# Attention weights kept in PSUM for every mixing sum, and the last sums placed between output chunks, in a two-layer mixer

## What is computed

```
# layer 0
att   = softmax(mlp(cond))                       # 64 x 8
agg_w = einsum('bk,koi->boi', att, weight)       # a 32x32 channel mixer per sample
y     = agg_w @ x + att @ bias_k                 # mix channels
r     = y @ base_w.T + base_b + 2 * lora(y, top-2 gates of 8)
x     = x + r
# layer 1: 9-tap grouped conv over features, plus (cond @ c_weight.T) and a
# bias, then a LoRA with top-2 gates of 4
x     = x + delta
```

## Time and profile before

| | us |
|---|---|
| median of 3 runs (199.12 to 201.44) | 199.79 |
| profiled execution, its own time | 199.16 |
| span of the profiled execution | 197.4 |
| PE busy (share of span) | 177.6 (90%) |
| DVE busy | 130.0 (66%) |
| ACT busy | 82.8 (42%) |
| POOL busy | 86.1 (44%) |

### The profile page before, as it was taken

One profiled execution on the slowest core, in us unless ns is written; L12 is line 12 of the kernel. 1 busy time (PEld: TensorE's weight loads), 2 busy tenths in 40 slices (PEclk: granted clock), 3 DMA queues, 4 the chain that ended last, 5 costly groups with the idle time before them and its releaser, 6 DMA issues.

```text
span 197.4 us, 3002 instructions
## 1 busy us (share of the span) xinstructions
PE 177.6 (90%) x1087; PEld 160.9 (81%) x1087; DVE 130.0 (66%) x251; ACT 82.8 (42%) x184; POOL 86.1 (44%) x86
## 2 busy tenths in 40 slices
PE   7999996504999899999999999999999999988991
PEld 7888886304888679999888999998889999987980
DVE  1496999996289844368877543688776753387573
ACT  3776595022082350773152517731523555126010
POOL 7023579920006672895300728952002796046000
PEclk9999999955699999999999999999999999999999
DMA  6997000001310014000002200000023000000225
GB/s 179 315 365 294 0 2 0 3 0 40 121 54 0 0 41 146 29 0 3 0 0 106 110 0 2 0 3 0 0 106 110 2 0 0 3 0 0 108 106 212
DMA packets 6350, 12.15 MB, mean 62 GB/s; under 512 B 704, under 2 KB 1088, under 8 KB 6336
## 3 DMA queue, kind: packets, MB, share of 16 engines
q1 hardware_dynamic: 6192, 11.84, 17.0%
q10 hardware_dynamic: 144, 0.13, 0.3%
HBM read 7.77 MB, written 4.19 MB: 61 GB/s over the span
## 4 chain that ended last, share of the span: by engine, by line
PE 69%; DVE 22%; ACT 3%; issue 3%; DVEq 0%; POOL 0%; ACTq 0%; POOLq 0%
PE ps L884 16%; PE ps L886 15%; PE ps L885 15%; PE ps L964 7%; DVE x1T L633 6%; PE ps L906 6%; PE ps L877 2%; DVE xs L722 2%; PE ps L961 2%; DVE xsl L627 1%; DVE late L637 1%; PE ps L1053 1%; DVE outb L710 1%; PE ps L923 1%; DVE above L609 1%
## 5 line engine op out<-in xcount | busy, mean ns | idle before, releaser
L884 PE MATMUL ps<-base_h,xTh 128*128 128x512 f32 x64 | 26.1, 408 | 0.0
L326 POOL TENSOR_TENSOR x1Tl<-x1T,x1Th 128x512 fp32r<-128x512 f32 x12 | 16.4, 1375 | 20.5 <-DVE lw L652 20.5
L886 PE MATMUL ps<-base_h,xTl 128*128 128x512 f32 x64 | 25.2, 394 | 0.0
L885 PE MATMUL ps<-base_l,xTh 128*128 128x512 f32 x64 | 25.2, 394 | 0.0
L668 DVE SCALAR_TENSOR_TENSOR x1T<-ps,side_s,xT_s 128x512 f32<-128x512 f32 x16 | 11.9, 750 | 17.0 <-PE ps L886 17.0
L310 POOL TENSOR_TENSOR xTl<-xT_s,xTh 128x512 fp32r<-128x512 f32 x12 | 15.0, 1275 | 17.2 <-ACT xTh L394 17.2
L964 PEld LDWEIGHTS ps<-mixT,p 128*128 128x128 f32 x128 | 18.9, 209 | 3.2 <-ACT p L407 1.7
L315 POOL TENSOR_TENSOR zl<-outb,zh 128x340 fp32r<-128x340 f32 x15 | 14.6, 972 | 13.5 <-ACT zh L419 13.4
L964 PE MATMUL ps<-mixT,p 128*128 128x128 f32 x128 | 19.2, 295 | 1.3 <-ACT p L407 1.3
L681 DVE TENSOR_TENSOR outb<-ps,s_sb 128x340 f32<-128x340 f32 x16 | 8.2, 510 | 17.3 <-PE ps L886 14.2
L961 PE MATMUL ps<-row_b,row_w 72*128 72x512 f32 x16 | 7.1, 442 | 10.0 <-DVE x1T L668 10.0
(11 more groups left out here) (182 smaller groups left out, 489.8 us busy)
## 6 DMA issues: line engine op xcount, KB each, us to landing
xT_s<-in_xT_dram SPq DMA_DIRECT2D x16, 256.0 KB, 4.7
out_dram<-outb SPq DMA_DIRECT2D x16, 256.0 KB, 2.3
x1T<-in_wT_dram SPq DMA_DIRECT2D x4, 256.0 KB, 6.5
x1T<-in_az_dram SPq DMA_DIRECT2D x1, 680.0 KB, 8.6
outb<-in_tapw_dram SPq DMA_DIRECT2D x1, 576.0 KB, 9.4
lgw_s<-in_lgw_dram SPq DMA_DIRECT2D x1, 272.0 KB, 3.4
...
```

Source lines behind the costliest of these rows:

```text
L326: nc.gpsimd.tensor_tensor(lo, full, hi.bitcast(F32), ALU.subtract).then_inc(x1_lo, 1)
L884: nc.tensor.matmul(dst, sh, mh, start=start and c == 0, stop=False)
L885: nc.tensor.matmul(dst, sh, ml, start=False, stop=False)
L886: last = nc.tensor.matmul(dst, sl, mh, start=False, stop=stop and c == n - 1)
```

## The change

Five things:

1. The attention weights stay in PSUM (now bank 7, `attb_b`); the copy `attb_s` is gone, and all mixing sums read PSUM. Other small products move to other banks or columns, the base sums to bank 1.
2. Mixing sum 1 moves behind `lwT_low(0)`. Sums 2 and 3 are each done in two halves of 512 results, through the tile `above`; the halves of sum 2 stand before `make_x1(0, 0)`, those of sum 3 between `make_x1(0, 0)`, `(0, 1)` and `(0, 2)`.
3. On PE the base sums move from behind chunks 2 and 3 of `x_base(0)` to ahead of them; the context product moves to the start, and the wait for the base sums' low part moves ahead of `x_logits(1, 1)`. `mix_logits(0)` now waits for both bias copies (`mixb_ok`, `ctx_ok`).
4. Loads: `side` ahead of the base weights, `az` ahead of `lbT` and of group 1's x. POOL's `uw_l` waits for `lb_lo` in place of `lw_ok`.
5. In group 1, ACT and DVE take `p0_out`, `lwT_high` and `lwT_low` ahead of part of the sums' splitting.

The diff, cut to its core:

```diff
-        attb_s = sb("attb_s", [P, TT, K0])
...
+        prod_half = above[:, 0:TG // 2 * C * K0].rearrange("p (t o k) -> p t o k", t=TG // 2, o=C)
...
-        HID, ATT, ATTT, ATTB, MXB, LGS, BSUM, CTXB, PSUMB = 7, 6, 7, 6, 7, 5, 7, 7, 7
+        HID, ATT, LGS, BSUM = 7, 6, 5, 1
+        attT_b = ps[0:K0, 6, 0:NB]
+        mixb_b = ps[:, 6, 0:NB]
+        ctx_b = ps[:, 6, NB:2 * NB]
+        attb_b = ps[:, 7, 0:TT * K0]
+        psum_b = ps[:, 7, 0:PJ]
...
+        MIX_STEPS = (1, 2, 4, 6)
+        attb = attb_b.rearrange("p (t k) -> p t k", k=K0)
...
+            sp.dma_start(side_s[:, :], side).then_inc(in_side, 16)
             for c in range(DC):
                 sp.dma_start(wT_s[:, c, :], wT[:, c, :]).then_inc(in_base[c], 16)
-            sp.dma_start(side_s[:, :], side).then_inc(in_side, 16)
+            sp.dma_start(az_s, az).then_inc(in_az, 16)
             sp.dma_start(lbT_s, lbT).then_inc(in_lb, 16)
             for c in range(DC):
                 load_xT(1, c)
-            sp.dma_start(az_s, az).then_inc(in_az, 16)
...
-            pool.wait_ge(lw_ok, 1)
+            pool.wait_ge(lb_lo, 1)
...
-            act.wait_ge(attb_mm, 1)
-            nc.scalar.activation(attb_s[:, :, :].rearrange("p t k -> p (t k)"), ps[:, ATTB, 0:TT * K0],
-                                 ACT.Copy).then_inc(attb_ok, 1)
...
-            gate_exp(0, gate0, dif0_ok, ex0_ok)
             act.wait_ge(dif_ok, 2)
             nc.scalar.activation(vw_h[:, :, :], ud, ACT.Copy).then_inc(suv_hi, 1)
+            gate_exp(0, gate0, dif0_ok, ex0_ok)
+            act.wait_ge(bsum_mm, 1)
+            nc.scalar.activation(row_w[:, :], ps[:, BSUM, :], ACT.Copy).then_inc(bsum_hi, 1)
             act.wait_ge(in_tap, 16)
             nc.scalar.activation(tap_h[:, :, :].rearrange("p k c -> p (k c)"), tapw_s, ACT.Copy).then_inc(tap_hi, 1)
             act.wait_ge(in_b1, 16)
             nc.scalar.activation(b1_h[:, :], b1T_s, ACT.Copy).then_inc(b1_hi, 1)
             for t in range(TG):
                 p0_out(0, t)
-            act.wait_ge(bsum_mm, 1)
-            nc.scalar.activation(row_w[:, :], ps[:, BSUM, :], ACT.Copy).then_inc(bsum_hi, 1)
...
             p0_out(1, 0)
+            p0_out(1, 1)
             sums_high(0, 0)
             sums_high(0, 1)
-            p0_out(1, 1)
-            sums_high(0, 2)
-            sums_high(0, 3)
             p0_out(1, 2)
             lwT_high(1)
             p0_out(1, 3)
+            sums_high(0, 2)
+            sums_high(0, 3)
...
-            def mix_sum(g, attb):
-                prod = prods[min(g, 1)]
-                if g == 1:
-                    dve.wait_ge(base_lo, DC)
-                nc.vector.tensor_tensor(prod, attb[:, TG * g:TG * (g + 1), :].unsqueeze(2).to_broadcast([P, TG, C, K0]),
-                                        wrep_s[:, :, :].unsqueeze(1).to_broadcast([P, TG, C, K0]),
+
+            def mix_sum(step, prod, t0, n):
+                nc.vector.tensor_tensor(prod, attb[:, t0:t0 + n, :].unsqueeze(2).to_broadcast([P, n, C, K0]),
+                                        wrep_s[:, :, :].unsqueeze(1).to_broadcast([P, n, C, K0]),
                                         ALU.mult).then_inc(prod_ok, 1)
-                dve.wait_ge(prod_ok, g + 1)
-                nc.vector.reduce_sum(agg[:, TG * g:TG * (g + 1), :], prod, AX_X).then_inc(agg_ok, 1)
+                dve.wait_ge(prod_ok, step)
+                nc.vector.reduce_sum(agg[:, t0:t0 + n, :], prod, AX_X).then_inc(agg_ok, 1)
+
+            def mix_half(g, half):
+                step = MIX_STEPS[g - 1] + half + 1
+                dve.wait_ge(agg_ok, step - 1)
+                mix_sum(step, prod_half, TG * g + half * TG // 2, TG // 2)
...
+            dve.wait_ge(ctx_mm, 1)
...
+            dve.wait_ge(in_side, 16)
+            for j in range(BT):
+                rows = slice(j * C, (j + 1) * C)
+                last = nc.vector.tensor_scalar(ctxbias[rows, :], ctx_b[rows, j:NB:BT],
+                                               side_s[rows, S_FS:S_FS + 1], None, ALU.add)
+            last.then_inc(ctx_ok, 1)
             for t in range(TG):
                 logits(0, t)
...
-            dve.wait_ge(agg_ok, 1)
-            mix_sum(1, attb_s)
             dve.wait_ge(bsum_hi, 1)
             minus(row_w[64:96, :], ps[64:96, BSUM, :], row_w[64:96, :]).then_inc(bsum_lo, 1)
             lwT_low(0)
-            for g in (2, 3):
-                dve.wait_ge(agg_ok, g)
-                mix_sum(g, attb_s)
-            dve.wait_ge(ctx_mm, 1)
-            dve.wait_ge(in_side, 16)
-            for j in range(BT):
-                rows = slice(j * C, (j + 1) * C)
-                last = nc.vector.tensor_scalar(ctxbias[rows, :], ps[rows, CTXB, j:NB:BT],
-                                               side_s[rows, S_FS:S_FS + 1], None, ALU.add)
-            last.then_inc(ctx_ok, 1)
-            dve.wait_ge(agg_ok, G)
+            dve.wait_ge(base_lo, DC)
+            mix_sum(2, prods[1], TG, TG)
+            mix_half(2, 0)
+            mix_half(2, 1)
             dve.wait_ge(suv_lo, 3)
-            for c in range(DC):
-                make_x1(0, c)
+            make_x1(0, 0)
+            mix_half(3, 0)
+            make_x1(0, 1)
+            mix_half(3, 1)
+            make_x1(0, 2)
+            make_x1(0, 3)
+            dve.wait_ge(agg_ok, MIX_STEPS[G - 1])
...
+            lwT_low(1)
             sums_low(0, 2)
             sums_low(0, 3)
-            lwT_low(1)
...
-                if i == 0:
-                    pe.wait_ge(attb_ok, 1)
-                elif t == 0:
+                if i and t == 0:
                     pe.wait_ge(lwT_lo, i)
...
-                    if i == 0:
-                        pe.wait_ge(bsum_lo, 1)
...
+            pe.wait_ge(in_side, 16)
+            nc.tensor.matmul(ctx_b, side_s[:, S_CTX:S_CTX + P], early_s[:, A_COND:A_COND + NB],
+                             start=True, stop=True).then_inc(ctx_mm, 1)
             pe.wait_ge(lgsum_ok, 1)
             for t in range(TG):
                 x_base(0, t, (0,))
             for t in range(TG):
                 x_base(0, t, (1,))
-            pe.wait_ge(prod_ok, 1)
+            pe.wait_ge(mixb_ok, 1)
+            pe.wait_ge(ctx_ok, 1)
             for t in range(TG):
                 mix_logits(0, t)
-            for c in range(2, DC):
-                for t in range(TG):
-                    x_base(0, t, (c,))
-            pe.wait_ge(mixb_ok, 1)
+            pe.wait_ge(base_lo, DC)
             for n, part in enumerate((base_h, base_l)):
                 for c in range(DC):
                     last = nc.tensor.matmul(ps[:, BSUM, :], ones_r[:, :], part[:, c, :],
                                             start=n + c == 0, stop=n == 1 and c == DC - 1)
             last.then_inc(bsum_mm, 1)
+            for c in range(2, DC):
+                for t in range(TG):
+                    x_base(0, t, (c,))
             turn_lw(0)
             x_logits(1, 0)
+            pe.wait_ge(bsum_lo, 1)
             x_logits(1, 1)
-            pe.wait_ge(bsum_lo, 1)
-            pe.wait_ge(in_side, 16)
-            nc.tensor.matmul(ps[:, CTXB, 0:NB], side_s[:, S_CTX:S_CTX + P], early_s[:, A_COND:A_COND + NB],
-                             start=True, stop=True).then_inc(ctx_mm, 1)
             make_y(0)
-            pe.wait_ge(ctx_ok, 1)
             pe.wait_ge(in_az, 16)
+            pe.wait_ge(prod_ok, MIX_STEPS[G - 1])
             for m in range(2):
```

More of the change, by code:

```diff
@@ L461, in mix_place @@
             def mix_place(g):
-                act.wait_ge(agg_ok, g + 1)
+                act.wait_ge(agg_ok, MIX_STEPS[g])
                 for j in range(BT):
@@ L485, in _ @@
             act.wait_ge(attT_mm, 1)
-            nc.scalar.activation(attT[:, :], ps[0:K0, ATTT, 0:NB], ACT.Copy).then_inc(attT_ok, 1)
+            nc.scalar.activation(attT[:, :], attT_b, ACT.Copy).then_inc(attT_ok, 1)
             x_high(0, 2)
@@ L529, in _ @@
             act.wait_ge(pjsum_mm, 1)
-            nc.scalar.activation(pj_sum[:, :], ps[:, PSUMB, 0:PJ], ACT.Copy).then_inc(pjsum_ok, 1)
+            nc.scalar.activation(pj_sum[:, :], psum_b, ACT.Copy).then_inc(pjsum_ok, 1)
             for t in range(TG):
```

18 lines of the change are left out of this document (8 added, 10 removed).

## The result

| | before | after |
|---|---|---|
| median of 4 runs on one chip, us | 199.45 (198.37 to 201.44) | 185.35 (184.84 to 185.81) |
| ratio after/before, 95% interval | | 0.9309, 0.9254 to 0.9364 |
| profiled execution, span, us | 197.4 | 183.7 |
| its own time, us | 199.16 | 185.67 |

The account below looks back on a forecast made before the run. PE was taken to wait 10.02 us for DVE, whose SBUF product is held by POOL, then to run at a low clock. 13.6 us there plus 1.1 at group 1 make 14.7 off 199.16: 184.7 us predicted, range 183.2 to 188.5.

Parts of the forecast that it names:

- the early stretch: PE up to the logits' end: 0.4 us for the context product, 0.4 us of wait (bounds 0 and 1.6).
- Which instructions are held: DVE beside POOL: instructions with both operands in SBUF are held; a PSUM product of 1024 takes 1.21 us.
- Rival B: DVE's PSUM products beside POOL are held like the others; only group 1's gain remains, 198.6 us; chance 0.04.
- DVE's list: DVE from ACT's lwTh at 29.3 us: lwTl 0.7, sum 1 2.5, two half sums 2.9; make_x1(0, 0) starts at 35.4.
- PE's chunks: Group 0's four output chunks: start 32.65 us, 1.87 us each, no gap, margins to DVE of 0.3 and 0 us.
- rival A: Chunks 2 and 3 of group 0: DVE misses PE by a little, 188 us, 191 with a lowered clock; chance 0.11.
- Gain up to the end of the chunks: Group 0's chunks end at 40.15 against 53.72 us, 13.6 us: 10.0 gap, 3.0 low clock and drain, 0.5 earlier start.
- signs of being wrong: A product beside POOL over 2 us, PE waiting over a us between chunks, or logits ending later than 33 us.
- Group 1's start: Ahead of group 1's first experts0: reordering removes PE's wait for ACT's tiles, 1.1 us won (bounds 0 and 1.8).
- Edits at no cost: Earlier base sums cost nothing; the removed ACT copy, reordered exponent and row_w are hidden.
- The sum: Whole kernel: 14.7 us off 199.16 gives 184.5, off the median 199.79 gives 185.1; predicted 184.7 us.

Follow-up runs that it names:

- sbuf_copy: The changed kernel with ACT's copy of the attention weights to SBUF put back and sums 1 to 3 reading it; 196.41 us, ratio 0.9915 to the kernel before.
- pool_later: The kernel before, with POOL starting group 1's bias rows and xTl only when mixing sum 3 is done; 193.45 us, ratio 0.9754.
- after_again: The changed kernel run once more without an edit; 185.56 us, ratio 0.9340 to the kernel before.
- after_third: The changed kernel run a third time without an edit, as a control; 185.80 us, ratio 0.9292 to the kernel before.
- whole_sums: The changed kernel with both halves of sum 3 ahead of make_x1(0,0); 189.11 us, ratio 0.9508 to the kernel before.
- before_again: The kernel before traced a second time without an edit; a single execution, 197.62 us, span 195.7 us.
- loads_back: The changed kernel with loads in their former order and POOL's uw_l waiting for lw_ok again; ratio 0.9263 without three slow runs, median of all six 186.69 us.
- early_y: The changed kernel with group 0's output chunk 0 waiting only for ACT's first logit copy, chunk 1 for the second; 185.29 us, ratio 0.9349.
- group1_back: The changed kernel with ACT's and DVE's order in group 1 as in the kernel before; median 187.72 us, ratio 0.9478, runs in two clusters.
- base_sums_back: The changed kernel with base sums behind chunks 2 and 3 of x_base(0) and row_w behind the base tiles again; 185.79 us, ratio 0.9362.

## Why the prediction was right

The mechanism was right and so were its large terms; one of them was in part lucky in the execution it was read from, and the early stretch was sized too small.

**Which instructions are held: right, and this decided everything.** The prediction read one row, `lwTl` at 0.69 us beside POOL's `xTl`, as the rule: a DVE instruction with one operand in PSUM isn't held, one with two in SBUF is. All five PSUM products took 1.22, 0.69 or 0.68 us. sbuf_copy gives the same instruction in the same place 10.70 us, and pool_later, with the operand left in SBUF and POOL moved, 1.21. Rival B (the PSUM products held as well, 198.6) needed a product of several us beside POOL; there is none. The Trainium skill (SBUF — State Buffer, Who interferes with whom) states that a DVE instruction with at most one SBUF input, outside the two-port modes, doesn't contend with GpSimd; the traces agree, by the 1.22 and 0.69 us above. The Trainium skill (VectorE: DVE Perf Modes, Rules for kernel authors) offers two ways for elementwise work on PSUM: to accept the rate of a PSUM source, or to copy to SBUF first if many operations follow. The second costs 12 us here: sbuf_copy is it. The changed kernel is the first, which the prediction didn't mention. Of the 62 cycles more for a PSUM source that the same page of the Trainium skill gives (The TRN2 errata) there is nothing in the rows: 1.22 against 1.22 us at 1024 results, 0.69 against 0.69 at 512.

**DVE's list: right within 0.2 us in its differences.** From ACT's `lwTh` to the first `make_x1` the prediction had 6.1 us (29.3 to 35.4); it was 36.23 - 30.31 = 5.9.

**PE's chunks: right, the margins larger than said.** 1.87 us a chunk was near (33.87 to 41.24 is 7.37 for four, 1.84 each). The start wasn't 32.65 but 33.87, with the slow start; 33.54 in after_again and 32.83 in after_third. DVE freed the first bank at 36.97 while PE wanted it at 37.59, a margin of 0.6 against the 0.3 said, the second at 38.94 against 39.41, 0.5 against 0. So rival A (DVE misses PE, 188 to 191) had some room before it. whole_sums makes it come true by another order, and 189.1 us lies between the 188 and 191 worked out for it.

**Gain up to the end of the chunks: 13.6 predicted; 12.5 in the first trace, 13.5 in after_third, 12.8 in after_again.** L1123 stood at 41.24, 40.20 and 40.90 us, predicted 40.15. The step that was mis-sized is the early stretch: the prediction took 0.4 us for the context product and 0.4 for a wait. Like for like, quick starts alone, the first base product comes 0.4 to 0.8 us later than in the kernel before (13.63 and 13.79 against 13.02 and 13.25). 0.24 of it is the context product now ahead of it, which the prediction counted (as 0.4). The rest is a wait for x, which it didn't: PE waits 0.54 us for x in after_again and 0.31 in after_third, and not at all in before_again. Why x comes later isn't shown: its loads for group 0 are issued first, at 1.72 us, in both load orders; in loads_back, with the old order, PE doesn't wait for it and the first base product starts at 13.40, but that is one trace. `ue` starts at 14.36 (first trace), 15.08 (after_again) and 14.42 us (after_third), against 13.3 to 14.2 said. The wait for `base_l`, held by `ue` as foreseen, was 0.59 us (after_again), 0.21 (early_y) and 0 (the first trace and after_third). And a slow start, which no trace of the kernel before showed, costs a further 1.2 to 1.4 us (14.98 against 13.79 and 13.63). So one of the prediction's own signs of being wrong came true: it named logits that end later than 33 us, and they end at 33.33 in the first trace, at 33.00 in after_again and at 32.30 in after_third.

**Group 1's start: 1.1 predicted, 1.33 measured.** The next thing late was `lwTl`, as said, by 0.22 us. The 14.96 us of this stretch are the same in after_again and after_third within 0.01. group1_back takes this part back and costs 3.4 us by the ratios (1.6 to 5.1 with both intervals), not 1.3, since in half of the executions the gaps seem to bring the lower clock with them. The prediction gave this part nothing for the clock, because the trace of before showed those gaps at 1.00.

**Edits at no cost: right for the base sums, open for the loads.** The place of the base sums and of `row_w` is worth nothing that these runs can tell (base_sums_back). For the load order the trace of loads_back shows nothing either, but three of its six runs are some 3 us longer. The removed copy on ACT was not tested by itself.

**The sum.** 184.7 against a median of 185.35. The difference, 0.65 us, is within the interval of the measurement (0.9254 to 0.9364 of 199.45 us is 184.6 to 186.8), so the medians alone ask for no explanation. For the profiled execution the sum was 184.5, its own time is 185.67: the chunks end 1.09 us later than said (41.24 against 40.15), with the slow start in it, group 1 gives 0.23 more than said, and 0.3 lies behind.

**What was lucky: the trace that the gain was read from.** The 13.6 us contain 1.56 us for `row_w` and the price of the low clock in two chunks. In before_again these are 0.98 and 0.96 us smaller. For the first the rows give the reason. DVE in the first trace of before, in the gating:

```profile
21.06 1.88 DVE L609 TENSOR_TENSOR above<-lgs 128x256 f32<-128x256 f32 x1
```

It takes 1.88 us in place of 0.42, beside POOL's `sw_l` (20.74 to 22.66 us). In before_again POOL's list is a us earlier, and the instruction in that place is held by 0.48 us only (0.89 in place of 0.41); all of DVE's list behind it moves with that. Had the prediction been made from before_again (197.62 us), its gain would have been near 12.7 us, and its forecast with 184.9 much the same, since the end of the chunks in the changed kernel was built up from its own list and not from the gap.

**A rival's price.** B put the time at 198.6 us if PSUM products were held too. sbuf_copy has the same hold, only from SBUF, and takes 196.41: its chunks end at 52.13 us and not near 54.2. B was priced about 2 us too high, which changed nothing here.
